# Norms, beta and block inversion of a delta rule moved from a stage of their own into the first stage

## The reference

```python
x = _layernorm(x + _L0_attn_ref(x, ...))      # phi(q) . cumsum(phi(k) v) / (phi(q) . cumsum phi(k)), then MLP
x = _layernorm(x + _L0_ffn_ref(x, ...))       # blocks of 32 values: maximum, scale, nearest grid value, @ wd.T
x = _layernorm(x + _L1_attn_ref(x, ...))

# in _L1_attn_ref, for 4 heads of 64:
q = silu(_causal_dwconv(hs @ Wq, conv_w_q))   # k and v likewise
beta = jax.nn.sigmoid(hs @ Wb)
# in _delta_chunkwise, for chunks of 32 tokens:
q, k = _l2norm(q), _l2norm(k)
kb = k * beta[..., None]
A = jnp.where(tri_lo_strict, kb @ jnp.swapaxes(k, -1, -2), 0.0)
inv = solve_triangular(eye + A, eye, lower=True, unit_diagonal=True)
# then the scan over chunks, gates, and Wo
```

## Time and profile before

| | |
|---|---|
| median of 3 runs | 5959.8 us (5956.16 to 5961.94) |
| span of the profiled execution | 5957.4 us |
| TensorE busy | 5355.5 us (90%) |
| VectorE busy | 4264.6 us (72%) |
| ScalarE busy | 2668.3 us (45%) |
| GpSimd busy | 2612.1 us (44%) |

### The profile page before, as it was taken

One profiled execution on the slowest core, in us unless ns is written; L12 is line 12 of the kernel. 1 busy time (PEld: TensorE's weight loads), 2 busy tenths in 40 slices (PEclk: granted clock), 3 DMA queues, 4 the chain that ended last, 5 costly groups with the idle time before them and its releaser, 6 DMA issues. The chain is left out here.

```text
span 5957.4 us, 119901 instructions
## 1 busy us (share of the span) xinstructions
PE 5355.5 (90%) x42776; PEld 4244.1 (71%) x42776; DVE 4264.6 (72%) x13841; ACT 2668.3 (45%) x6214; POOL 2612.1 (44%) x3780
## 2 busy tenths in 40 slices
PE   6999999999999999988966636999999999999987
PEld 5888888888888888867944424777777777777755
DVE  4777777777777777762238875888888888888871
ACT  2555555555555555542133322444444444444441
POOL 1222222222222222222277742666666666666660
PEclk8999999999999999998955556999999999999998
DMA  1011011011011011006755542222222222222211
GB/s 41 28 36 37 29 35 36 29 34 37 29 35 36 29 35 36 29 29 134 190 149 141 141 108 57 61 62 62 62 61 62 61 60 59 60 62 61 62 35 45
DMA packets 599702, 357.50 MB, mean 60 GB/s; under 512 B 336400, under 2 KB 589136, under 8 KB 599120
## 3 DMA queue, kind: packets, MB, share of 16 engines
q1 hardware_dynamic: 528656, 314.18, 18.9%
q10 hardware_dynamic: 65664, 16.78, 1.2%
q0 software_dynamic: 4800, 18.88, 1.1%
HBM read 212.59 MB, written 137.10 MB: 59 GB/s over the span
## 5 line engine op out<-in xcount | busy, mean ns | idle before, releaser
L526 POOL TENSOR_TENSOR a_shift<-a_mean_var,a_eps 128x2 f32<-128x2 f32 x256 | 71.3, 279 | 1834.9 <-DVE a_mean_var L736 1834.9
L2136 PE MATMUL c_bank<-c_xT,c_gate 128*128 128x512 f32 x1024 | 503.0, 614 | 0.7 <-ACT c_statsT L1889 0.7
L750 DVE SCALAR_TENSOR_TENSOR a_cv<-a_raw,a_taps,a_cv 128x256 f32<-128x256 f32 x1152 | 461.9, 479 | 19.5 <-ACT a_cv L628 10.0
L820 PE MATMUL a_bank<-a_w,a_hidden 128*128 128x256 f32 x2048 | 459.1, 382 | 0.9 <-ACT a_hidden L613 0.9
L918 PE MATMUL a_bank<-a_turned,a_w 128*128 128x256 f32 x2048 | 453.0, 379 | 1.1 <-ACT a_turned L574 1.1
L820 PEld LDWEIGHTS a_bank<-a_w,a_hidden 128*128 128x128 f32 x2048 | 383.8, 190 | 71.8 <-issue 20.6
L918 PEld LDWEIGHTS a_bank<-a_turned,a_w 128*128 128x128 f32 x2048 | 384.1, 190 | 51.2 <-ACT a_turned L574 1.6
L1786 POOL TENSOR_TENSOR c_expd<-c_e,c_logit 128x16 f32<-128x16 f32 x128 | 371.7, 2904 | 50.7 <-DVE c_logit L1972 37.9
L1772 POOL TENSOR_TENSOR c_stats<-c_l2sq,half 128x16 f32<-128x16 f32 x128 | 373.4, 2917 | 15.1 <-DVE c_l2sq L1961 15.1
L2140 PEld LDWEIGHTS c_bank<-c_statsT,c_gate_stats 128*128 128x128 f32 x2048 | 270.0, 192 | 124.9 <-issue 124.9
L1356 POOL TENSOR_TENSOR i_coef<-i_base,i_exponent 128x12 f32<-128x12 f32 x128 | 298.9, 2335 | 71.6 <-issue 52.8
(11 more groups left out here) (295 smaller groups left out, 14140.7 us busy)
## 6 DMA issues: line engine op xcount, KB each, us to landing
a_x<-in_x SPq DMA_DIRECT2D x64, 256.0 KB, 3.3
scratch_xb<-a_xb SPq DMA_DIRECT2D x64, 256.0 KB, 2.1
scratch_q<-a_qkv_rows SPq DMA_DIRECT2D x64, 256.0 KB, 2.2
scratch_k<-a_qkv_rows SPq DMA_DIRECT2D x64, 256.0 KB, 2.7
scratch_v<-a_qkv_rows SPq DMA_DIRECT2D x64, 256.0 KB, 3.0
b_window<-scratch_v SPq DMA_DIRECT2D x8, 2048.0 KB, 22.1
scratch_long<-b_out ACTq DMA_DIRECT2D x8, 2048.0 KB, 24.4
scratch_short<-b_out POOLq DMA_DIRECT2D x8, 2048.0 KB, 18.0
```

Source lines behind the costliest of these rows:

```text
L750: ins = dve.scalar_tensor_tensor(cv[s][:, n, c], raw[s][:, n, c, j:j + TOK], taps[:, n, c, j:j + 1], cv[s][:, n, c], ALU.mult, ALU.add)
L820: ins = pe.matmul(dst[:, t * D:(t + 1) * D], src[s][:, c, tile_cols(t)], weight[:, c], start=(c == 0), stop=(c == chunks - 1))
L2136: pe.matmul(dst[:].rearrange("p (h t) -> p h t", h=H), gate1[:, c, cols], xT[sl][:, c:c + 1].broadcast_to([P, H, P]), start=(c == 0), stop ...
```

## The change

`phase_i` goes away. Its work becomes stages of `phase_a`, for 256 tokens at a time:

- `beta`: TensorE multiplies `xbT`, which phase_a already has, with Wb; ScalarE copies the negative. `squares`: ScalarE squares the silu results, where they lie, into `cv`; VectorE sums. `powers`: GpSimd computes e to that value, adds 1, raises 24 values to -0.5, and scales `kn`. The sigmoid is thus made of powers. `kT`, `gram`, `keep`: as in phase_i, for two tiles; the sign of the mask is turned (`drop_block`), so that the inversion adds instead of subtracting.
- `gather`: once a sequence (8 tiles, one block a partition, so one set) the blocks come back from HBM twice, into `A` and `T`. `inverse0` to `inverse3`: in each of a sequence's 4 steps four pieces of the inversion, each of two columns, that is four operations on VectorE which wait for one another. Gather is due 34.2 units ahead of the first piece.
- The shares get the new stages; `beta` stands between `qkv1` and `conv`. `DEPTH` gives way to `PERIOD = 10.9`: the period in units of the shares was 47.79 / 4.779 = 10.0 and is now 10.9.
- Five buffers have one slot instead of two: phik_rows, phiq_own, v_own, resid, xa. What writes them gets a wait for the reader of the step before.
- SyncE stores the coefficients and blocks, gathers, and stores the inverses.

```diff
-    DEPTH = 4.779
+    PERIOD = 10.9
...
-              ("lnB_stats", 1.69), ("lnB", 1.72), ("xbT", 3.97), ("qkv1", 3.91), ("conv", 1.64), ("qkvT", 0.01)]
+              ("lnB_stats", 1.69), ("lnB", 1.72), ("xbT", 3.97), ("qkv1", 0.05), ("beta", 3.86), ("conv", 1.64),
+              ("qkvT", 1.2), ("squares", 1.2), ("powers", 2.8), ("kT", 0.6), ("gram", 0.5), ("keep", 1.6),
+              ("gather", 34.2), ("inverse0", 2.7), ("inverse1", 2.7), ("inverse2", 2.7), ("inverse3", 0.01)]
...
-    order = pipelined(shares, STEPS, DEPTH)
+    order = pipelined(shares, STEPS, sum(share for _, share in shares) / PERIOD)
...
-        v_own = slots("v_own", [P, T, H, STRIP], 2)
+        v_own = slots("v_own", [P, T, H, STRIP], 1)
...
             def values(i, s):
+                if not_first(i, s, 1):
+                    computed(act, *back(i, s, 1), "attn")
...
+            def powers(i, s):
+
+                pool.wait_ge(S["ssq_ready"], seq(i, s))
+                in_sbuf(pool, i, s, "beta")
+                if not_first(i, s, 2):
+                    pool.wait_ge(coef_stored[s % 2], 16 * uses(i, s, 2))
+                beta = base[s][:, :, 2]
+                link(pool.tensor_tensor(beta, e_base[:], beta, ALU.pow))
+                link(pool.tensor_tensor(beta, beta, one_base[:], ALU.add))
+                link(pool.tensor_tensor(coef[s][:], base[s][:], powers_half[:], ALU.pow))
+                pool.tensor_tensor(coef[s][:, :, 1], coef[s][:, :, 1], coef[s][:, :, 2], ALU.mult)\
+                    .then_inc(S["coef_ready"], 1)
...
+            def invert(piece):
+
+                def stage(i, s):
+                    m = s * PIECES + piece
+                    A_, T_ = A_sets[i % 2], T_sets[i % 2]
...
+                    for j in columns_of[m]:
+                        below_j = slice(j + 1, CUT)
+                        shape = [P, j, CUT - 1 - j]
+                        part = product[:, 0:shape[1] * shape[2]].rearrange("p (c r) -> p c r", c=j)
+                        link(dve.tensor_tensor(part, A_[:, j:j + 1, below_j].broadcast_to(shape),
+                                               T_[:, 0:j, j:j + 1].broadcast_to(shape), ALU.mult))
+                        rest = T_[:, 0:j, below_j]
+                        ins = dve.tensor_tensor(rest, rest, part, ALU.add)
...
-        phase_i(nc, w, k, scratch, batches, banks)
```

More of the change, by code:

```diff
@@ L370, in phase_a @@
         shift = slots("shift", [P, 4, T], 4)
+        base = slots("base", [P, T, 3, HEADS], 2)
+        coef = slots("coef", [P, T, 3, HEADS], 2)
+        powers_half = sb("powers_half", [P, T, 3, HEADS])
+        e_base = sb("e_base", [P, T, HEADS])
+        one_base = sb("one_base", [P, T, HEADS])
+        kn = slots("kn", [P, T, D], 1)
+        kT = slots("kT", [P, PAIRS, TOK], 1)
+        below = slots("below", [P, T, HEADS, CUT], 2)
+        drop_block = sb("drop_block", [P, CUT])
+        A_sets = [sb(f"A{n}", [P, CUT, CUT]) for n in range(2)]
+        T_sets = [sb(f"T{n}", [P, CUT, CUT]) for n in range(2)]
+        product = sb("product", [P, SIDE // 4])
         rden = slots("rden", [P, T, H], 2)
@@ L429, in _ @@
             def _(dve):
+                for b in range(BLOCKS):
+                    rows = slice(b * CUT, (b + 1) * CUT)
+                    dve.tensor_tensor(drop_block[rows], k["ident"][rows, rows], k["keep_causal"][rows, rows], ALU.subtract)
                 dve.wait_ge(landed, 16 * len(loads))
@@ L518, in _ @@
                 sp.wait_ge(qkv_stored[m], 48 * batches * STEPS // OUTS)
+            for m in range(2):
+                sp.wait_ge(coef_stored[m], 16 * batches * STEPS // 2)
+                sp.wait_ge(inverse_stored[m], 16 * (batches // 2))
         @block.gpsimd
@@ new lines, in keep @@
+            def keep(i, s):
+                if not_first(i, s, 2):
+                    dve.wait_ge(below_stored[s % 2], 16 * T * uses(i, s, 2))
+                for o in range(2):
+                    src = full(dve, i, s, f"G{o}")
+                    ins = dve.tensor_tensor(below[s][:].rearrange("p t (r o) j -> p o (t r) j", o=2)[:, o],
+                                            src[:, 0:T * PAIRS * CUT].rearrange("p (n j) -> p n j", j=CUT),
+                                            drop_block[:, None, :].broadcast_to([P, T * PAIRS, CUT]), ALU.mult)
+                    freed(ins, s, f"G{o}")
+                in_sbuf(dve, i, s, "G0")
+                in_sbuf(dve, i, s, "G1")
+                dve.sem_inc(S["below_ready"], 1)
@@ L761, in _ @@
             stages = {
+                "squares": sums, "keep": keep,
                 "ln1_stats": norm_stats(0, x_sb, S["ln1_var"], True),
```

414 lines of the change are left out of this document (148 added, 266 removed).

## The result

| | before | after |
|---|---|---|
| median | 5960.9 us (5956.2 to 5964.3) | 6962.4 us (6958.1 to 6964.9) |
| span of the profiled execution | 5957.4 us | 6959.8 us |
| TensorE busy in it | 5355.5 us | 5576.4 us |
| VectorE busy in it | 4264.6 us | 4383.8 us |

A forecast was written before the change was run, and what follows sets the result against it. Phase_a was taken as bound by TensorE before, then by the engines' order: 5957.4 - 601.4 + 64 x (66.4 - 40.6) + 16 = 7023, with 2.4 to the median 7025 us; range 6620 to 7200.

The forecast's parts named there:

- Steps, 66.4 us: Forecast length of a phase_a step of 256 tokens: 60.2 us walked plus 3.3 and 2.9 for the clock; before 40.6.
- The walk: One phase_a step followed along the new engine order with measured durations and 0.1 us per hand-over: mean 60.2 us.
- item 7: Last part of a long phase_a step: attention half, kT, Wq, Wk, Wv, Wb, gram, `xd`; ends at 61.8 us.
- The clock, 6.2 us a step: TensorE's half clock after waits in phase_a: 3.3 us behind the attention's wait, 2.9 behind the 5.2 us wait.
- The tail: End of phase_a: the last batch's inversion, stored and gathered after all else, adds 16 us.
- (a): Rival: phase_a stalls as walked, clock hardly lost; 6630 us, to 6700 with half the clock's price; chance 15%.
- (b): Rival: the order costs half in phase_a, steps of 48 to 55 us, total 5850 to 6300 (to 6550); chance 8%.
- (d): Rival: clock low through idle zone and first MLP product, VectorE's chained operations slower; 70 us a step, over 7230; chance 8%.
- (c): Rival: new VectorE and GpSimd work fills VectorE's waits free, TensorE stays phase_a's bound; 5507 us; chance 4%.
- place 1: After the q, k, v projections and wo, only ffn (1.8 us) precedes `den`, which needs VectorE's key sums.
- place 2: VectorE's addition, `keep`, statistics and inversion piece stand before the key sums' end at 14.0; TensorE idles 5.2 us.
- place 3: In 3 of 4 steps quantisation stands between masks of tiles 0 and 1; attention's second half waits about 8 us.

The follow-up runs named there:

- the best order: Changed kernel with PERIOD = 9.8 and a second set of shares instead of 10.9 and its own: 5514.4 us, ratio 0.9254.
- the run with the filled wait: Changed kernel with fifteen unread products a step put on TensorE ahead of den's wait for the key sums: 6874.7 us, ratio 1.1531.
- The run for place 3: Changed kernel with shares of lnA and quant moved by 0.01, so tile 1's masks precede the quantisation in all four steps: 6889.3 us, ratio 1.1562.

## Why the prediction was right, point by point

- **phase_i gone, 601.4 us**: right, 599.4.
- **What bounds the step**: right. The order, not the amount of work: the sums by engine fitted under 43 us, and in a good order the same instructions take 42.1. TensorE's own time was put a little high, 42.7, since the 2.1 were added to the whole step of 40.6, of which TensorE is busy for 39.4 (976.45 of 1000 us); in the best order it is busy for 41.1.
- **Steps, 66.4 us**: measured 65.6 over the four quoted, 64.7 over all 63. In the terms of the forecast that is 41.1 of work, 16.6 of waits and 6.7 of slow products (64.4, and some short gaps), where 42.7, 17.5 and 6.2 were forecast. The walk's mean was taken with 61.3 us, while its item 7 ends at 61.8; with 61.8 the forecast would be 0.4 a step and 24 us higher. Times 64, the 1.7 between 66.4 and 64.7 are 109 us. At 1608 against 1651 + 16, `phase_a` came out 59 shorter than forecast, so the ends of the stage gave some 50 back: filling and draining cost more than a tail of 16. These two misses have opposite signs, and so have those of the single waits below; that the total came within 63 us is in part luck.
- **The items**: `den` was to wait 5.2 and waits 7.0 (414.3 in 59); 2.1 us of VectorE's time there (120.5 in 58) is the wait for x that the walk didn't have. With the load early `den` waits 5.1 (81.0 in 16), as walked. The walk left SyncE's queue out: the load stands behind a store that waits for `keep`. The attention was to wait 8 in three steps of four and waits 5.4 (259.3 in 48). What is missing there stands one job earlier: the scores of tile 1 wait 3.1 us (185.1 in 59) for the masks of tile 0 on VectorE. I had walked these masks and put no wait of the scores down to them. The MLP product begins 4.8 us after `den` (4.3 walked), but the turns between them run slowly and fill that time, so its wait reads 1.1 and not 2.5. In the fourth step kT waits for GpSimd, as walked, by 2.9 us.
- **VectorE's pieces**: `keep` 0.49 for 0.6, the additions, statistics and masks within 0.1, the sums 1.39 (1.22 and 0.17) for 1.55. The convolution 9.13 for 7.2, hidden under TensorE's products, as the walk had it. The room of VectorE was read wrongly in one place: it waits for some 4 us once in a step of before, not twice (the rows at 1558.94 and 1599.56 are the same wait, one step apart). The sums, taken from the earlier trace rows, don't hang on it.
- **The clock, 6.2 us a step**: the size was right. TensorE was busy for 47.8 us a step in after (738.92 us in 15.45 steps) and for 41.1 in the best order (976.50 in 23.75), so 6.7 us of slow products. The split was not. Behind the attention's wait 3.3 was expected in a long step; in the step quoted above the attention's second half, kT and Wq lost 0.85, 0.49 and 0.46, that is 1.8 (in the next long step 0.86, 0.49 and 1.59, that is 2.9). Behind `den`'s wait, with 2.9 expected, `den`, two turns and the MLP product lost 0.8, 0.45, 0.45 and 2.0, that is 3.7. Another 1.4 was not in the walk: the attention's first half and the state product ahead of it (1.94 for 1.08, 1.19 for 0.61), behind the waits for the masks of the first tile. Together that makes 6.9 in this step. The rule that was weighed, of the Trainium skill (TensorE: Matmul & The Clock Gate, section "HAM oscillation — how this bites in real kernels"), says that the slow start comes again with every such wait. The trace agrees: `den` is slow (1.84 or 1.85 us) in 58 of the 59 steps from 300 to 4200 us, and the first MLP product in all of them (8.9 to 9.7).
- **Single buffers, nothing**: right, 1.0002 in the order of before.
- **The tail**: the 7.16 us for the gathered blocks and 22 us of inversion stand uncovered between the last blocks at 4281 and 4312, then the stores; TensorE idles for 39.05 (8.41 before). The 22 were said to stand mostly in the walk's drain; in after they do not.
- **The rivals**: (a) no price for the clock falls to the run with the filled wait. (b), steps of 48 to 55 us, did not come. Nor did (d), over 70 us a step: the first MLP product takes 8.9 to 9.7 us, where twice its 7.07 would be 14, so the clock is low in a part of it only, and the second one takes 7.07. (c), 5507 us, was named as the other side. It is what a good order makes of this work: 5514. The change as such was sound, its period and shares were not.

What stays open: no run undoes place 1 or place 2 alone, so how the loss divides between them isn't shown. The run for place 3 shows why single repairs say little here: the next late job takes over.

## What to carry to other kernels

Where an order is fixed by a table, a change of its period moves every stage against every other, and added stages come in between them; walk one step along each engine's queue with measured durations, the DMA queues among them, before trusting sums per engine. A repair of one wait is worth only the distance to the next late job (73 us for a wait of 5.4 us in three steps of four), so change the order as a whole and look for the one without waits. Durations are part of this: a short instruction may take many times as long beside another engine's, so the walk's durations hold for their order only. If a change loses, run it once more in two other orders before judging its idea: here the same instructions took 5514 to 6962 us.

## What the runs showed of the hardware

**The convolution's slow instructions.** The 18 operations took 7.21 us before and 9.13 after. Their count, then the shortest, median and longest in ns, from 1000 to 2000 us, first of before and then of after:

```profile
L750 DVE SCALAR_TENSOR_TENSOR a_cv<-a_raw,a_taps,a_cv x450: 471/479/485, 1018.3 to 1997.2; 128x256 f32<-128x256 f32 x150
```
```profile
L877 DVE SCALAR_TENSOR_TENSOR a_cv<-a_raw,a_taps,a_cv x270: 385/473/1490, 1042.7 to 1968.7; 128x256 f32<-128x256 f32 x135
```

The median is the same and the longest is three times as long. The timeline from 2096.0 to 2098.4 shows two of them, which take 2.89 us, and what GpSimd does then:

```profile
2095.73 2.89 DVE L877 SCALAR_TENSOR_TENSOR a_cv<-a_raw,a_taps,a_cv 128x256 f32<-128x256 f32 x2
```
```profile
2095.42 1.51 POOL L604 TENSOR_TENSOR a_x<-a_x 128x512 f32<-128x512 f32 x1
2097.01 1.33 POOL L605 TENSOR_TENSOR a_x<-a_x,a_b 128x512 f32<-128x512 f32 x1
```

The two run beside GpSimd's two operations and end at 2098.62, 0.3 us after the second. In the step of the earlier trace rows GpSimd had no work while the convolution ran. The mean of the 18 is 479 ns before and 581 after. The kernel before with the period of after shows 582 too, without any new work on GpSimd, and the changed kernel at period 10.0, with all of that work, shows 479 (the other orders 579 to 611). So it is the order that puts the two beside each other. The Trainium skill (SBUF — State Buffer, section "Who interferes with whom") says that a VectorE instruction with two inputs from SBUF contends with a GpSimd instruction that reads SBUF, and calls the ports that they share an exclusive lock. The trace agrees: 1.4 us for 0.47. No run separates this by itself.

**A small product of GpSimd held up by a row of VectorE's.** The other way round it is larger. GpSimd multiplies 8 values (L626) in 0.20 us; the shortest, median and longest in ns from 1000 to 2000 us, first at period 10.0 and then with the masks first:

```profile
L626 POOL TENSOR_TENSOR a_coef<-a_coef x19: 203/204/205, 1036.5 to 1981.4; 128x8 f32<-128x8 f32 x19
```
```profile
L626 POOL TENSOR_TENSOR a_coef<-a_coef x15: 258/464/4801, 1058.2 to 1952.9; 128x8 f32<-128x8 f32 x15
```

In after it takes 2.0 us in the median, where nobody waits for it in three steps of four. The long ones run beside the quantisation, whose operations VectorE issues back to back, several of them with two inputs from SBUF, and last until its end (4.36 us from 2021.29, the quantisation's last operation ending at 2025.44). That it is the same contention is argued from this, not shown by a run of its own.

**Useless products make it faster.** Fifteen added products a step gave 88 us back, through the clock (`den` 1.06 for 1.85 us).
